# Heads 4 and 5 of a sixth sample transposed by DMA, and the weight chunks of the next pair moved behind them

## The reference

```
q, k, v = x Wq, x Wk, x Wv          # 32 query heads, 8 key heads, 128 wide
q, k = rope(rmsnorm(q)), rope(rmsnorm(k))
k_all = [k_cache[pages], k]; v_all = [v_cache[pages], v]   # 512 cached keys + 128 new = 640
probs = softmax(mask(q k_all^T / sqrt(128)))
out = x + (probs v_all) Wo
```

## Time and profile before

| | |
|---|---|
| median of 3 runs | 1276.88 us (1274.43 to 1278.03) |
| profiled execution | 1275.63 us |
| its span | 1273.9 us |
| busy: PE, DVE, ACT, POOL | 1257.2, 913.3, 785.6, 826.7 us |
| granted clock of TensorE | full speed in all 40 slices |
| DMA | 190.41 MB, mean 149 GB/s |

### The profile page before, as it was taken

The page is one execution under the profiler, slowest core; times in us unless marked ns, Lnnn a source line. Parts: engine busy times, 40 slices in busy tenths (PEclk is TensorE's granted clock), DMA queues, the critical chain, the costliest instruction groups (busy, mean ns, idle before and its releaser), DMA issues.

```text
span 1273.9 us, 25215 instructions
## 1 busy us (share of the span) xinstructions
PE 1257.2 (99%) x6553; PEld 1076.1 (84%) x6553; DVE 913.3 (72%) x2658; ACT 785.6 (62%) x1850; POOL 826.7 (65%) x810
## 2 busy tenths in 40 slices
PE   9999999998999999999999999999999999999998
PEld 8888877877888888888888888888888888888886
DVE  6532357778877777887777788777777887777774
ACT  5731333637666668676666676766667767666664
POOL 2110011338778888687888887877887869788863
PEclk9999999999999999999999999999999999999999
DMA  8321224277667678755676787567777775667744
GB/s 290 115 83 38 84 71 142 60 262 211 126 132 160 148 142 228 189 130 129 145 157 153 157 223 193 128 136 146 161 159 201 170 199 128 135 155 151 156 101 83
DMA packets 356912, 190.41 MB, mean 149 GB/s; under 512 B 302402, under 2 KB 321218, under 8 KB 356546
## 3 DMA queue, kind: packets, MB, share of 16 engines
q1 hardware_dynamic: 337824, 136.32, 46.1%
q10 hardware_dynamic: 11410, 33.69, 8.1%
q0 software_dynamic: 7568, 19.14, 6.7%
HBM read 119.71 MB, written 16.91 MB: 107 GB/s over the span
## 4 chain that ended last, share of the span: by engine, by line
PE 86%; DVE 6%; issue 4%; DMA 3%; ACT 2%; ACTq 0%; POOL 0%; DVEq 0%; POOLq 0%
PE bank L1697 18%; PE tail L1737 14%; PE wide L1767 14%; PE tail L1804 13%; PE wide L464 4%; PE wide L544 3%; PE bank L1720 3%; PE wide L1731 3%; PE bank L464 3%; PE tail L464 3%; PE wide L599 2%; DMA spread<-one_over_denominators 1%; PE bank L544 1%; PE bank L599 1%; DVE tail L2270 1%
## 5 line engine op out<-in xcount | busy, mean ns | idle before, releaser
L1737 PE MATMUL tail<-prT,vt 128*128 128x512 f32 (+1 forms) x975 | 251.0, 400 | 0.2
L1737 PEld LDWEIGHTS tail<-prT,vt 128*128 128x128 f32 x975 | 173.1, 189 | 36.3 <-DVE prT L2221 5.2
L1804 PE MATMUL tail<-woT,oT 128*128 128x512 f32 x768 | 179.6, 390 | 0.9 <-DVE oT L2274 0.9
L1804 PEld LDWEIGHTS tail<-woT,oT 128*128 128x128 f32 x768 | 144.1, 188 | 31.1 <-DVE oT L2274 1.3
L1767 PE MATMUL wide<-kT,qT 128*128 128x320 f32 x512 | 159.4, 311 | 2.0 <-DVE mx L2250 1.7
L1767 PE MATMUL wide<-kT_low,qT 128*128 128x320 f32 x512 | 158.3, 309 | 0.0
L1767 PE MATMUL wide<-kT,qT_low 128*128 128x320 f32 x512 | 158.1, 309 | 0.0
L1354 POOL TENSOR_TENSOR tick<-tick 128x1 f32<-128x1 f32 x255 | 53.1, 208 | 154.9 <-DMA turned<-parts 47.1
L1993 ACT ACTIVATE raw<-raw,nm,q_scale 128x640 f32<-128x640 f32 x124 | 114.6, 925 | 61.1 <-DVE nm L2253 59.0
L1412 POOL TENSOR_TENSOR parts<-raw,parts 128x1280 f16<-128x1280 f32 x55 | 145.7, 2649 | 8.0
L2250 DVE CUSTOM_DVE_ANT_0 raw<-wide,bias 128x640 f32<-128x640 f32 x124 | 101.7, 820 | 27.4 <-issue 26.9
(11 more groups left out here) (308 smaller groups left out, 3040.2 us busy)
## 6 DMA issues: line engine op xcount, KB each, us to landing
w_ring<-pair_weights SPq DMA_DIRECT2D x80, 256.0 KB, 4.3
k_raw<-k_pages SPq DMA_DIRECT2D x512, 32.0 KB, 1.8
v_raw<-v_pages SPq DMA_DIRECT2D x512, 32.0 KB, 2.7
spread<-one_over_denominators ACTq DMA_DIRECT2D x32, 512.0 KB, 4.2
xTb<-x_transposed ACTq DMA_DIRECT2D x31, 512.0 KB, 3.9
rope<-rope_tables SPq DMA_DIRECT2D x31, 256.0 KB, 3.3
out<-y POOLq DMA_DIRECT2D x31, 256.0 KB, 4.3
w_raw<-w_gate_up SPq DMA_DIRECT2D x10, 512.0 KB, 3.5
```

Source lines behind the costliest of these rows:

```text
L1737: last = nc.tensor.matmul(tail[g][:, first * S:end * S], vt[v_part][:, j, g * D:(g + 1) * D], prT[p_part][:, first:end, j, :], start=(j == ...
L1804: last = nc.tensor.matmul(place[:, :], oT[:, g, o_part, (h % REP) * S:(h % REP + 1) * S], woT[w_part][:, h, :], start=(h == o_part == w_pa ...
```

## The change

Sample 6 joins `THIRDS`, so the turn b = 7 has a back unit with a third. On SP, in the turn b = 7, the values come in two lots with the third's transposes between them, as in the other turns with a third, and the first 8 chunks come behind the first lot and these transposes; chunks 12 to 15 come behind the values of b = 0. `EARLY["next"]` is spread otherwise. POOL takes no chunk ahead of the key split in turn b = 7; in the first two turns of the kernel it takes the output's chunks in other lots, and the first turn's second parts of probs (`make_rest`) go from DVE to POOL. On DVE the mask of the keys comes ahead of the low probs; in late turns the root's steps are (1, 1, 2) behind masks 0, 1, 2, and `normalise(1)` comes behind mask 3. On ACT, the spread is issued behind the key copy in the kernel's second turn also, and the first unit's `high_turned` moves from its front turn into the next, behind the squares.

```diff
-    EARLY = {"next": ((0, 1), (2,), (3, 4), (5, 6, 7)), "out": ((), (), (12, 13, 14), (15, 16, 17)), None: ((),) * 4}
+    EARLY = {"next": ((), (0,), (1, 2, 3), (4, 5, 6, 7)), "out": ((), (), (12, 13, 14), (15, 16, 17)), None: ((),) * 4}
-    THIRDS = range(2, 6)
+    THIRDS = range(2, 7)
...
 def halve(u, before, n, k, first_turn, rest_too):          # POOL
             pool.wait_ge(s_exp, u * HP + HALF * (k + 1))
+            if k and not first_turn:
+                pool.wait_ge(s_norm, u * G)
...
 def turn(...):                                             # POOL
-            if extra == "next":
-                low_weights(own, 0, 2)
...
             if extra == "next":
-                low_weights(own, 2, 2 * KT)
+                low_weights(own, 0, 2 * KT)
...
-                halve(u, before, n, 0, True, False)
+                halve(u, before, n, 0, True, True)
...
+                if left:
+                    low_weights(own, left[1], NCHUNK)
...
             if first_turn:
-                low_weights(own, 3 * KT, 4 * KT)
+                low_weights(own, 3 * KT, LEFT[0])
                 pool.wait_ge(s_init[1], 16 * BLK)
-                low_weights(own, 4 * KT, LEFT[0])
-        LEFT = (NCHUNK - 2, NCHUNK)
+        LEFT = (4 * KT - 1, NCHUNK - 2)
...
 def run():                                                 # SP
                 turn_probs(pair, B - 2)
+                load_values(pair, B - 1, pages, 0, VALUES_FIRST)
+                turn_third(pair, B - 2)
                 load_weights(pair + 1, 0, NRING)
-                load_values(pair, B - 1, pages)
+                load_values(pair, B - 1, pages, VALUES_FIRST)
                 load_weights(pair + 1, NRING, 3 * KT)
...
                 load_keys(pair + 1, 0, pages, KEYS_FIRST)
-                load_weights(pair + 1, 3 * KT, 4 * KT)
                 load_values(pair + 1, 0, pages)
-                load_weights(pair + 1, 4 * KT, NCHUNK)
+                load_weights(pair + 1, 3 * KT, NCHUNK)
...
 def turn(...):                                             # ACT
                 squares(1, 0, REP)
                 if back and not share:
+                    high_turned(u, before_back, 0, True)
+                if back and not share:
...
-            if back and not third:
+            spread_late = front and (third or not share)
+            if back and not spread_late:
                 spread_shares()
...
                 high(0, 3, kT[:, :, L:NK], ...)
+            if back and spread_late:
+                spread_shares()
...
-                    if back and h == 0:
+                    if back and h == (REP if second_queries_late(pair, b, front, back) else 0):
                         copy_values(1)
...
-                high_turned(n, before_front, 0, not back)
+                if back:
+                    high_turned(n, before_front, 0, False)
...
 def turn(...):                                             # DVE
+                mask_keys()
                 if not back:
-                    mask_keys()
                     dve.wait_ge(s_keyno, 4)
...
                 low_new()
-                if front:
-                    mask_keys()
...
                 for h in range(HP):
+                    if late and h == 0:
+                        dve.wait_ge(c_free[1], before[1] + 3 + FIRST)
                     mask_max(h)
-                    if back and h == 0:
+                    if back and h == (3 if late else 0):
                         normalise(1)
-                    if late and h < 4:
-                        if h == 0:
-                            dve.wait_ge(c_free[1], before[1] + 3 + FIRST)
-                        next(second_root, None)
+                    if late:
+                        for _ in range((1, 1, 2)[h] if h < 3 else 0):
+                            next(second_root, None)
...
-                    if not back and h == HALF + 1:
-                        for i in range(HALF):
-                            rest_of(i)
```

More of the change, by code:

```diff
@@ L1318, in turns @@
                 turn(pair, last + 3, before(last + (pair * B + 3)), True, True, True, None, True, True)
-            turn(pair, 6, before(pair * B + 6), True, True, True, None, True, True)
             more = pair + 1 < NPAIR
@@ L1516, in run @@
             LOOP = BEGUN + CARRIES + 1
-            SIXTH = LOOP + THIRD_CARRIES * (len(THIRDS) - 1)
-            SEVENTH = SIXTH + CARRIES + 1
+            SEVENTH = LOOP + THIRD_CARRIES * (len(THIRDS) - 1)
+            AFTER = SEVENTH + CARRIES + 1
             def middle(pair):
@@ L1523, in middle @@
                     turn(pair, b + 3, b * THIRD_CARRIES + (pair * NCARRY + LOOP), b + 1, b + 4)
-                turn(pair, 6, pair * NCARRY + SIXTH, 4, 7)
             with pool.Fori(0, NPAIR - 1) as pair:
@@ L1528, in run @@
                 turn(pair, B - 1, pair * NCARRY + SEVENTH, B - 3, 0, "next")
-                turn(pair + 1, 0, pair * NCARRY + (SEVENTH + CARRIES), B - 2, 1)
-                turn(pair + 1, 1, pair * NCARRY + (SEVENTH + 2 * CARRIES), B - 1, 2, "out")
+                turn(pair + 1, 0, pair * NCARRY + AFTER, B - 2, 1)
+                turn(pair + 1, 1, pair * NCARRY + (AFTER + CARRIES), B - 1, 2, "out")
             pair = NPAIR - 1
@@ L1533, in run @@
             turn(pair, B - 1, pair * NCARRY + SEVENTH, B - 3, None)
-            n = pair * NCARRY + (SEVENTH + CARRIES)
+            n = pair * NCARRY + AFTER
             add_share(NPAIR * B - 2, B - 2, n)
@@ L1635, in run @@
                 load_unit(7, pair, 2)
-                with sp.Fori(0, len(THIRDS)) as b:
+                with sp.Fori(0, len(THIRDS) - 1) as b:
                     load_unit(2, pair, b + 3)
@@ L1661, in run @@
                 load_unit(5, NPAIR - 1, b + 3)
-            load_unit(9, NPAIR - 1, B - 1)
             turn_probs(NPAIR - 1, B - 1)
@@ L2074, in turn @@
                 if third and ahead:
-                    load_x(b + 1)
+                    load_x((b + 1) % B if isinstance(b, int) else b + 1)
             early(0)
@@ L2087, in turn @@
                 high(0, 3, kT[:, :, L:NK], bank[0][:, 0:G * S].rearrange("p (g c) -> p g c", g=G))
+            if back and spread_late:
+                spread_shares()
             if third:
-                spread_shares()
                 high_turned_third()
```

## The result

| | median | runs |
|---|---|---|
| before, on the same chip | 1277.32 us | 4 |
| after | 1307.98 us (1304.44 to 1315.74) | 4 |

The ratio is 1.0253 [1.0226, 1.0280]: slower by 2.5%, where 0.6% was forecast, and beyond the range. The profiled execution has a span of 1302.7 us, 28.8 more than before.

The account below looks back on a forecast made before the run. TensorE was taken as the bound, busy 1257.2 of 1273.9 us. Terms +18.7 - 5.0 - 3.8 - 2.0 = +7.9 on the profiled 1275.63 gave 1283.5, plus 1.25 for the median: 1284.8 us, range 1267 to 1293.

Parts of the forecast that it names:

- part 6: On DVE, key mask ahead of low probs: into gaps over 1 us, elsewhere 0.1 us late; 0 to 1 us, taken as 0.
- part 3: In turn b = 7, ACT's copies wait for weight chunk 0; TensorE delayed 6.2 us (4.1 to 8.4) at each of three boundaries.
- 1: ten transposes fewer, four turns: Turn b = 7 of four pairs: ten TensorE transposes fewer, worth 1.25 us each, 5.0 us won.
- 2, 3: ACT's wait, three turns: Turn b = 7: SP issues chunk 0 later, at 494.4, ACT waits for it; 18.7 us lost at three boundaries.
- 4: turns behind turn 7: Late turns, DVE: root ahead of mask 3 and normalise 1, 1.6 us earlier against a 0.96 wait; 3.8 us won.
- 5: up to the fourth turn: Kernel's second turn: ACT copies moved behind squares and key copy, with the root step's 0.96; 2.0 us won (0.5 to 4).
- L: Time when weight chunk 0 lands in turn b = 7 at the first pair boundary; forecast 498.8, bounds 496.7 to 501.
- rival A: Turn b = 7: chunk 0 lands at 497.2, without x load and backlog; each delay 4.6, total +3.0, 1280 us; chance 0.14.
- Rival B: Turn b = 7: ACT is not held for chunk 0; delays of 1 us give 1269, none 1266; chance 0.16.
- Rival C: Spread, issued about 502.6 among chunks and pages, also lands late; first mask 3.8 us late, +11, 1296 us; chance 0.10.

## Why the prediction was right or wrong

**The step that failed is part 6**, "the key mask moves ahead of the low probs on DVE: in third turns into a gap of over 1 us in front of them, in others 0.1 us late at most (11 turns: 0 to 1 us; I take 0 ...)". It cost 15.4 us in after, and 7.4 when moved alone. The gap was there; the duration wasn't. I took 0.48 us from the old place, where POOL was mostly idle beside it, and carried it to a place where POOL isn't, and so the term of 0 had the wrong mechanism: what counts is not the gap ahead of the low probs but the POOL work beside the mask, which held it for 8.62 us. Without this step the change measures 1292.57, inside the range, though still 7.8 above the forecast.

**The next is a term that part 3 doesn't have.** "Nothing gives it back" was right, but the delay was priced as idle time alone. TensorE's clock fell behind each such stretch, and three turn 7s lost 10.8 us to it (9.8 with the mask back; in pair 0, 4.28 for 2.81, so 1.5 of it stands behind the mask's stall). The earlier trace rows had the clock at 1.00 throughout, which said only that no such stretch had been there.

Point by point, against the 20.9 us by which the span's change (28.8) exceeds the sum (7.9):

| term | sum | measured in after | difference |
|---|---|---|---|
| 1: ten transposes fewer, four turns | -5.0 | -5.0: last turn 7 28.24 to 26.99; the others hold it by 160 matmuls for 170 | 0 |
| 2, 3: ACT's wait, three turns | +18.7 | 4.61 + 4.84 + 4.89 = 14.3 | -4.4 |
| clock behind it and behind the mask | none | 4.28 + 3.54 + 2.95 | +10.8 |
| mask in pair 0's turn 7 | 0 | 4.75 | +4.75 |
| 4: turns behind turn 7 | -3.8 | +2.4; -2.8 with the mask back, so the mask is 5.2 of it | +6.2 |
| 5: up to the fourth turn | -2.0 | -1.5 | +0.5 |
| the pairs' second and third turns | 0 | +1.7; +0.4 with the mask back | +1.7 |
| a third turn of the last pair | 0 | 31.13 for 29.89 | +1.2 |

These come to 20.8.

1. The third's worth, 1.25 a turn: right to the hundredth in the last pair (28.24 to 26.99, and 26.98 in the kernels with the mask back and with the chunks last).
2. SP's order: its first chunk went out at 492.63, 494.0 in before's time, for 494.4 forecast. The landing was too high: 2.9 to 3.1 us for the first chunk, where I took 4.4 from the chunks behind other transposes. L was 497.1 and not 498.8. That is rival A's number, and its doubt about today's 4.6 was the right one. Of its two reasons the x load is the likelier: in the kernel with all chunks first they go out right behind the prob transposes, as before, but 2.6 us ahead of the x load and not beside it, and the first lands in 3.1. The other figure of part 3, 2.6 us, was nearer than 4.4, though what the Trainium skill ("DMA: Bandwidth & Descriptors", Anatomy of one DMA) fits are DMAs issued from GpSimd, and the chunks are issued from SP; by the sum there it gives L = 497.0, not 496.9.
3. The mechanism was right in place and order: ACT idle 4.27 at L1920, the queries' copy behind it, TensorE idle ahead of both transposes and of the group 1 value sums. The first of these waits was 1.86, for 3 to 4 forecast, as chunk 0 was there 1.7 earlier. Each delay was 4.6 to 4.9, forecast 6.2, and 4.6 by A. The chunks at the last place took those waits away.
4. The late root: q_scale's wait is gone in every kernel with the new steps. The turns behind turn 7 gained 2.8 with the mask out of the way (31.72 and 31.74, "near 31.3" forecast), so 3.8 was a third too high; in after the mask took 2.55 in each of them, and in the first TensorE waited 1.28 for the low probs.
5. The second turn: 2.36 by the fourth turn in the kernel without sample 6, 1.23 with the mask back, 2.0 forecast.

Rival B, by which ACT isn't held, did not occur: ACT stood 4.27 us for chunk 0. Rival C did not occur in after: the spread was issued at 498.84, ahead of the place I had for it, and TensorE doesn't wait for a maximum for more than 0.5 us. It shows only where the chunks are last.

One stall stands apart: a third turn of the last pair is 1.2 longer in after and 1.84 in the kernel with the mask back. With the mask back TensorE waits 0.58 there for ACT's last copies of probs and 0.77 for POOL's copy of `turned_third`; in after it waits 0.5 for ACT's. POOL stood 1.1 us for that data in the kernel with the mask back. Why it came late in that one turn stays open, and the waits are not the whole of the excess.

## What to carry to other kernels

A moved instruction doesn't bring its duration with it: look at what POOL does at the new place, and also at the old one when POOL's work moves. Price a new stall of TensorE by its idle time and then by what runs at the lower clock behind it, here two thirds as much again (9.8 against 14.8 us with the mask back). Before a transfer is put ahead of another, see what else is in flight: no order of 2 MB of weights and two transposes that was tried made the kernel faster, though the mask's stalls stand in most of these runs, and the parts that left turn 7 alone were the ones that paid.

## What the runs showed of the hardware that was not expected

- A tensor_scalar of 128x512 (int16 to float32), 0.48 us alone, took 8.62 us beside eight POOL instructions in a row, 9.7 in the kernel with all chunks first and 10.5 in the one with two chunks first; with an accumulator written beside it 0.74 us, whatever POOL did.
- The granted clock fell to 0.50 behind three idle stretches close together (1.9, 1.9 and 0.8 us in pair 0 of after, 1.9, 2.1 and 0.8 in pair 1, 1.9, 2.4 and 0.6 in pair 2). It stayed there through 5.8 and 3.5 us of work in turn 7 of pairs 1 and 2 of after, and in pair 0 through 3 us before the mask's stall and 4.3 behind it. In the kernel with the chunks last and the mask's other form, stalls of 0.68, 2.27 and 1.21 us with 3.4 us of work between one and the next left it at 1.00.
- Two DMA transposes behind 2 MB of weights and seven pages held SP's queue for 7.22 us and landed after 10.7 to 12.0; with only the pages in front (after) it was 3.50 and 3.4 to 4.2.
